# Layer norms centred on VectorE alone, attention weights loaded from ScalarE's queue, unread products at two places of the first layers

## The chip, the cores and the metric

One NeuronCore of a Trainium2 chip. The kernel is one program on one core; the metric is the time of one execution in microseconds, median over runs. All data is fp32 unless said otherwise.

## What is computed

x is 8 images of 64 channels, 16x16 pixels. Cut from the reference:

```python
x = L0(x)   # non-local block: theta, phi, g by 1x1 products (phi, g max-pooled 2x2)
            # f = softmax(theta^T phi); y = f g; w_y = Ww y; batch norm of w_y; + x
x = L1(x)   # sign(x+b11) conv 3x3 with sign weights, bn, + x, prelu;
            # sign, conv 1x1 with sign weights, bn, + , prelu
t = to_tokens(x)                      # 8 x 256 tokens of 64
t = t + attention8(ln(t))             # 8 heads, softmax, Wu, + bu
t = t + moe(ln(t), 8 experts, top 2)  # gelu
t = t + haar_attention(ln(t))         # keys by pinv(W_Q), rotary, Haar far field
t = t + moe(ln(t), 16 experts, top 2) # silu(h1) * h2
ln(v) = (v - mean(v)) / sqrt(var(v) + 1e-5)     # over the 64 of a token
```

## The kernel before

Each engine runs a program of its own, written out by hand, and the engines meet at semaphores. Nothing is scheduled: an engine's order is the order of its code, and an instruction that waits holds all behind it. The images lie in pairs on the 128 partitions (x0, 128x1024); the tokens in T, 16 tiles of 128 tokens by 64, on 128 partitions.

**The first layers (0 to 42 us).** SP issues all loads one after another: w0, x, vec, wwT, the conv weights (w3T, w1T, w3n, w1n), the loads for the pseudo-inverse (nsA, nsAT), consts (with the identity for transposes), then the five attention weights wqT, wkT, wvT, wu, bu on one semaphore `attn_loaded`, then the rest. TensorE computes w0 times x (L1204, four products of 512 columns; an fp32 product is two records in the trace), theta times phi (L1212), gw (L1220), then the fold of wkT and wqT (L1226, eight products into bank 7, behind `attn_loaded`), the transposes of f_prob (L1235), the wy products (L1242), five unread products (`keep_clock`, L836, 128x512 bf16 on the sign weights w3s), a join of the batch norm's halves (L1250), the fold of wvT and wu (L1254), eight more unread products, and the 3x3 conv (L1262). ScalarE: theta (L690), the sign weights (L697, L698), two exponentials (L702), two copies AH of the fold (L707), the copy of the first transposes (L710), wy (L713). VectorE: the softmax of f up to f_prob (L1482), sums of the conv weights (L1486 to L1489), the copy of the second transposes (L1491), AL from the fold (L1495), the counts of wy for the batch norm (L1500). GpSimd zeroes tiles first: phi, gw, sgn, w3s, w1s, then `zeros` (128x128).

**The layer norms.** There are four (n = 0 to 3), ahead of each attention and each expert layer, all by `layer_norm` on VectorE with helpers. VectorE takes the statistics of the 16 tiles (L1594), makes the mean (L1602) and the variance (L1603, L1604), and centres tiles 0 to 7 (L1605) while `ln_pool` on GpSimd centres tiles 8 to 15 (L478). ScalarE takes the square root (L600), VectorE the reciprocal (L1607) and multiplies the 16 tiles in four pieces (L1612), the third of which waits for GpSimd. TensorE transposes them piece by piece. In the first norm GpSimd then adds bu to T (L572). `step` makes VectorE wait for its own instruction.

Of the kernel before, what the change touches and what calls it, by code (L numbers as in the profile page):

```python
# [24 lines left out]
ALU = mybir.AluOpType  # L25
# [3 lines left out]
P = 128  # L29
B, C, IMG = 8, 64, 16  # L30
# [7 lines left out]
EXP2, EXP3, HID = 8, 16, 128  # L38
# [102 lines left out]
def hybrid_kernel(nc, io, out):  # L141
    ctx = ExitStack()
    with ctx:
# [5 lines left out]
        def S(name):  # L149

            if name not in sems:
                sems[name] = ctx.enter_context(nc.semaphore(name))
            return sems[name]
# [29 lines left out]
        wqT = from_early(C, HEADS * C).rearrange("p (h m) -> p h m", h=HEADS)  # L183
        wu = from_early(C, HEADS * C).rearrange("p (h m) -> p h m", h=HEADS)
# [226 lines left out]
        def _(sp):  # L411
            def load(dst, src, name):
                sp.dma_start(dst, src).then_inc(S(name), 16)
# [3 lines left out]
            load(vec[:], io["vec"], "vec_loaded")  # L417
            load(wwT[:], io["wwT"], "ww_loaded")
            load(w3T[:], io["w3T"], "l1_loaded")
# [7 lines left out]
            load(consts[:], io["consts"], "consts_loaded")  # L427
            load(wqT[:], io["wqT"], "attn_loaded")
            load(wkT[:], io["wkT"], "attn_loaded")
            load(wvT[:], io["wvT"], "attn_loaded")  # L430
            load(wu[:], io["wu"], "attn_loaded")
            load(bu[:], io["bu"], "attn_loaded")
            load(wq3[:], io["q3"], "l3_loaded")
# [39 lines left out]


        def ln_pool(gp, n):

            gp.wait_ge(S("ln_mean"), n + 1)
            gp.tensor_tensor(xn[:, 8:16], T[:, 8:16], lnc[:, 1, 8:16].unsqueeze(2).broadcast_to([P, 8, C]),  # L478
                             ALU.subtract).then_inc(S("ln_centred"), 1)

# [68 lines left out]
        @block.gpsimd  # L549
        def _(gp):  # L550
            gp.memset(phi[:], 0.0).then_inc(S("blocks_zeroed"), 1)
            gp.memset(gw[:], 0.0).then_inc(S("blocks_zeroed"), 1)
            gp.memset(sgn[:], 0.0).then_inc(S("pads_zeroed"), 1)
            gp.memset(w3s[:], 0.0).then_inc(S("pads_zeroed"), 1)
            gp.memset(w1s[:], 0.0).then_inc(S("pads_zeroed"), 1)
            gp.memset(zeros[:], 0.0).then_inc(S("zeros_ready"), 1)
            gp.wait_ge(S("zeros_ready"), 1)
            gp.memset(ones64[:], 1.0).then_inc(S("ones_ready"), 1)
            gp.memset(first_row[:], 0.0).then_inc(S("zeros_ready"), 1)
            gp.wait_ge(S("zeros_ready"), 2)  # L560
            for o in range(2):
                gp.memset(first_row[C * o:C * o + 1, o, :], 1.0).then_inc(S("ones_ready"), 1)
                gp.wait_ge(S("ones_ready"), o + 2)
            gp.memset(b2two[:], 0.0).then_inc(S("b2_zeroed"), 1)
            gp.memset(gates[:], 0.0).then_inc(S("gates_zeroed"), 1)

            gp.wait_ge(S("attn_loaded"), 80)
            ln_pool(gp, 0)
            gp.wait_ge(S("ln_normalised"), 4)
            for u in range(2):  # L570
                t8 = T[:, 8 * u:8 * u + 8, :]
                gp.tensor_tensor(t8, t8, bu[:].unsqueeze(1).broadcast_to([P, 8, C]),  # L572
                                 ALU.add).then_inc(S("t_biased"), 1)
            attention_pool(gp)
            ln_pool(gp, 1)
            ln_pool(gp, 2)
            l3_pool(gp)
            ln_pool(gp, 3)

            gp.wait_ge(S("f3_hid_ready"), CHUNKS)  # L580
            for kk in range(CHUNKS, CHUNKS * EXP3):
                e, c = kk // CHUNKS, kk % CHUNKS
                slot, filled = gate_slot(3, e)
                gp.wait_ge(S(f"gate_row{slot}_{c // 2}"), 16 * filled)
                gp.wait_ge(S("f3_glu"), kk + 1)
                gp.tensor_tensor(hid[kk % RING], hid[kk % RING], gate_rows[slot][:, c * CHUNK:(c + 1) * CHUNK],
                                 ALU.mult).then_inc(S("f3_hid_ready"), 1)
# [96 lines left out]
        def _(act):  # L684
            act.preload_act_table(ACT.Exp)
            act.wait_ge(S("vec_loaded"), 16)

# [4 lines left out]

            act.wait_ge(S("l1_loaded"), 64)
            act.wait_ge(S("pads_zeroed"), 3)
# [138 lines left out]
        def keep_clock(pe, bank, products):  # L833

            for _ in range(products):
                pe.matmul(ps[:, bank, :], w3s[:, 0, :], w3s[:, 4:8, :].rearrange("p k m -> p (k m)"), start=True, stop=True)  # L836
# [361 lines left out]
        @block.tensor  # L1198
        def _(pe):
            pe.wait_ge(S("l0_loaded"), 32)  # L1200

# [15 lines left out]
            pe.wait_ge(S("pg_ready"), 1)  # L1217
            pe.wait_ge(S("ww_loaded"), 16)
            for j in range(J):
# [3 lines left out]

            pe.wait_ge(S("attn_loaded"), 80)
            for h in range(HEADS):
                mm = pe.matmul(ps[:, 7, h * C:(h + 1) * C], wkT[:, h, :], wqT[:, h, :],  # L1226
                               start=True, stop=True)
            mm.then_inc(S("folded"), 1)

            pe.wait_ge(S("consts_loaded"), 16)  # L1230
# [8 lines left out]
            for j in range(J):  # L1239
# [4 lines left out]
                if j % 2 == 1:  # L1244
                    mm.then_inc(S("wy_ready"), 1)

            pe.wait_ge(S("wsign_ready"), 4)
            keep_clock(pe, 2, 5)
            pe.wait_ge(S("bn_halves"), 1)
            pe.matmul(ps[:, 6, 0:2], con("halfavg"), col[:, 0:2], start=True,  # L1250
                      stop=True).then_inc(S("bn_joined"), 1)

            for h in range(HEADS):
                mm = pe.matmul(ps[:, 3, h * C:(h + 1) * C], wvT[:, h, :], wu[:, h, :],  # L1254
                               start=True, stop=True)
# [182 lines left out]
        def _(dve):  # L1438
# [3 lines left out]
            def wide(c, n=C, t=TILES):  # L1442

                return c.unsqueeze(2).broadcast_to([P, t, n])
# [36 lines left out]
            for q in halves:  # L1481
                tt(f_prob[:, q], f_exp[:, q], wide(f_col[:, 2, q], t=8), ALU.mult).then_inc(S("f_prob_ready"), 1)  # L1482
            dve.wait_ge(S("l1_loaded"), 64)
            ones = [("w3n", w3n, 9 * C, 20), ("w1n", w1n, C, 21)]
# [104 lines left out]
            def layer_norm(n, after_first=None):  # L1589
# [11 lines left out]
                step(tt(lnc[:, 3, :], lnc[:, 1, :], lnc[:, 1, :], ALU.mult))  # L1601
                ts(lnc[:, 1, :], lnc[:, 0, :], 0.5, None, ALU.mult).then_inc(S("ln_mean"), 1)  # L1602
                step(stt(lnc[:, 4, :], lnc[:, 3, :], C / 4.0, lnc[:, 2, :], ALU.mult, ALU.add))  # L1603
                ts(lnc[:, 5, :], lnc[:, 4, :], 1.0 / C, EPS_LN, ALU.mult, ALU.add).then_inc(S("ln_var"), 1)  # L1604
                step(tt(xn[:, 0:8], T[:, 0:8], wide(lnc[:, 1, 0:8], t=8), ALU.subtract))  # L1605
                dve.wait_ge(S("ln_std"), n + 1)
                step(dve.reciprocal(lnc[:, 7, :], lnc[:, 6, :]))  # L1607
                for p in range(4):
                    q = slice(CT * p, CT * p + CT)
                    if p == 2:  # L1610
                        dve.wait_ge(S("ln_centred"), n + 1)
                    tt(xn[:, q], xn[:, q], wide(lnc[:, 7, q], t=CT), ALU.mult).then_inc(S("ln_normalised"), 1)  # L1612
# [248 lines left out]
```

## Time and profile before

| | |
|---|---|
| median of 3 runs | 397.25 us (395.0 to 397.92) |
| the profiled execution | 399.14 us |
| its span (first to last instruction) | 397.4 us |
| mean granted TensorE clock | 0.914 |
| busy: PE, PEld, DVE, ACT, POOL | 347.0, 237.8, 272.3, 211.7, 165.9 us |
| instructions | 7115 |

PE is TensorE's matmuls, PEld its weight loads, DVE VectorE, ACT ScalarE, POOL GpSimd, SPq SP's queue. A timeline row gives start and duration in us, then engine, line, operation, output <- input, and shapes; neighbours of one kind are merged (x8), and a bracket tells the idle time before it and what ended it. Full TensorE clock (1.0) is 2.4 GHz, 0.5 is 1.2 GHz.

### The profile page before, as it was taken

To read this page: it belongs to the slowest core of one execution; us is meant where nothing else is said; L and a number is where in the kernel's file an instruction comes from. 1 tells how busy PE (TensorE), PEld (TensorE's weight loads), DVE (VectorE), ACT (ScalarE), POOL (GpSimd) and SP (SyncE) were. 2 spreads that over 40 slices of the span, in tenths; PEclk is the share of its full clock that TensorE was granted. 3 is DMA by queue.
4 is the path that set the end of the run, shared out by engine and by line. 5 is a ranking of instruction groups with operands and counts; after the bars stand their busy time and mean duration, and the time that the engine had idled before them with its cause. 6 is when DMAs were issued, how large, how long until landed. Compare 5 with 4: busy or idle time off the path is not lost. (4 is left out here: it accounts for less than half of the span.)

```text
span 397.4 us, 7115 instructions
## 1 busy us (share of the span) xinstructions
PE 347.0 (87%) x2438; PEld 237.8 (60%) x2438; DVE 272.3 (69%) x657; ACT 211.7 (53%) x523; POOL 165.9 (42%) x175
## 2 busy tenths in 40 slices
PE   4786389999999999999769999858467899999996
PEld 1552266888888888887454233346055666666662
DVE  1878777888888888877383664687895655555541
ACT  1555358777777677878527444360324344444440
POOL 5000135455455545555310000140110299999995
PEclk9988559999999999999977999985578999999999
DMA  6944000000000000000000991000000946665531
GB/s 175 236 99 163 0 0 1 2 2 2 1 2 2 1 2 2 2 1 2 0 2 10 338 357 44 2 0 2 0 0 15 316 156 216 208 194 192 206 107 53
DMA packets 16436, 30.92 MB, mean 78 GB/s; under 512 B 5968, under 2 KB 9744, under 8 KB 16400
## 3 DMA queue, kind: packets, MB, share of 16 engines
q1 hardware_dynamic: 16400, 30.46, 23.9%
q8 instruction: 20, 0.33, 0.3%
q14 instruction: 16, 0.13, 0.1%
HBM read 29.73 MB, written 0.72 MB: 77 GB/s over the span
## 5 line engine op out<-in xcount | busy, mean ns | idle before, releaser
L524 POOL TENSOR_TENSOR va_vb<-va_vb,rowinv 128x512 f32<-128x512 f32 x64 | 66.6, 1041 | 70.1 <-DVE rowinv L1681 70.1
L649 ACT ACTIVATE va_vb<-ps,negmax 128x256 f32<-128x256 f32 x128 | 59.8, 477 | 8.0 <-DVE negmax L1674 7.8
L776 ACT ACTIVATE wy<-ps 128x512 f32<-128x512 f32 x64 | 38.1, 597 | 46.8 <-PE ps L1111 46.8
L1111 PE MATMUL ps<-XP,early 64*128 64x256 f32 x512 | 58.0, 380 | 1.5 <-DVE hid_g L1742 1.5
L1111 PEld LDWEIGHTS ps<-XP,early 64*128 64x128 f32 x512 | 46.6, 186 | 14.8 <-issue 5.5
L1674 DVE TENSOR_REDUCE negmax<-ps 128x2 f32<-128x512 f32 x64 | 44.1, 689 | 7.8 <-PE ps L912 7.6
L912 PE MATMUL ps<-keys_gates,xcur 128*128 128x256 f32 x256 | 47.9, 310 | 1.4 <-DVE keys_gates L1666 1.4
L478 POOL TENSOR_TENSOR xn<-T,lnc 128x512 f32<-128x512 f32 x4 | 4.2, 1042 | 105.7 <-DVE lnc L1602 105.7
L912 PEld LDWEIGHTS ps<-keys_gates,xcur 128*128 128x128 f32 x256 | 35.5, 195 | 13.8 <-issue 11.3
L923 PE MATMUL ps<-consts,va_vb 128*128 128x128 f32 x256 | 39.2, 276 | 2.8 <-POOL va_vb L524 2.3
L939 PE MATMUL ps<-pT,vproj 128*64 128x256 f32 x256 | 34.5, 392 | 0.0
L923 PEld LDWEIGHTS ps<-consts,va_vb 128*128 128x128 f32 x256 | 30.3, 148 | 6.7 <-POOL va_vb L524 4.2
L640 ACT ACTIVATE keys_gates<-ps 128x512 fp32r<-128x512 f32 x32 | 19.2, 600 | 27.2 <-PE ps L889 27.1
L649 ACT ACTIVATION_READ_ACCUMULATOR va_vb<-ps,negmax 128x1 f32 x128 | 26.5, 207 | 0.0
L1666 DVE TENSOR_TENSOR keys_gates<-ps,keys_gates 128x512 fp32r<-128x512 f32 x32 | 22.1, 691 | 3.7 <-ACT keys_gates L640 2.6
L633 DVE COPY pT<-ps 128x512 f32<-128x512 f32 x32 | 21.8, 682 | 1.9 <-PE ps L923 1.9
L1767 DVE TENSOR_TENSOR theta_qk<-ps,wy 128x512 f32<-128x512 f32 x16 | 11.1, 692 | 14.1 <-ACT wy L776 14.1
L939 PEld LDWEIGHTS ps<-pT,vproj 128*64 128x64 f32 x256 | 15.6, 136 | 7.6 <-issue 1.4
L1681 DVE RECIPROCAL rowinv<-rowsum 128x2 f32<-128x2 f32 x64 | 10.6, 166 | 13.7 <-ACT va_vb L649 13.3
L1051 PE MATMUL ps<-XP,w2raw 64*128 64x512 f32 x64 | 19.4, 688 | 0.0
L631 ACT ACTIVATE pT<-ps 128x512 f32<-128x512 f32 x32 | 19.3, 603 | 0.2 <-PE ps L923 0.2
L888 PE MATMUL ps<-xcur,AH 128*128 128x256 f32 x64 | 17.7, 297 | 0.1
(322 smaller groups left out, 684.5 us busy)
## 6 DMA issues: line engine op xcount, KB each, us to landing
pT<-gates_row SPq DMA_DIRECT2D x16, 512.0 KB, 4.8
vproj<-gates_row SPq DMA_DIRECT2D x14, 512.0 KB, 5.1
gate_row_keys<-gates_row SPq DMA_DIRECT2D x14, 512.0 KB, 4.9
early<-in_f_in SPq DMA_DIRECT2D x1, 2048.0 KB, 8.4
consts<-in_consts SPq DMA_DIRECT2D x1, 816.0 KB, 5.3
x<-in_x SPq DMA_DIRECT2D x1, 512.0 KB, 4.5
w2raw<-in_f_in SPq DMA_DIRECT2D x1, 512.0 KB, 4.0
out<-in_f_out SPq DMA_DIRECT2D x1, 512.0 KB
```

Of the source, the lines that this page charges most:

```text
L524: gp.tensor_tensor(prob[:, n % 4], prob[:, n % 4], rowinv[:, n % 4, :].unsqueeze(2).broadcast_to([P, U, N]), ALU.mult).then_inc(S("p_scale ...
L631: eng.activation(dst, src, ACT.Copy).then_inc(S("pT_even"), 1)
L633: eng.tensor_copy(dst, src).then_inc(S("pT_odd"), 1)
L649: ins = act.activation(prob[:, n % 4, u, :], ps[:, 1 + n % 2, u * N:(u + 1) * N], ACT.Exp, bias=negmax[:, n % 4, u:u + 1], accum_out=rowsu ...
L776: act.activation(act_out[:, kk % 2, :].rearrange("p (o n) -> p o n", o=2), ps[:, 2 * pair_of(kk):2 * pair_of(kk) + 2, 0:2 * P], ACT.Silu). ...
L912: mm = pe.matmul(ps[:, 1 + n % 2, u * N:(u + 1) * N], xcur[:, g, u * P:(u + 1) * P], K[:, k % 2, n % 2, :], start=(part == 0), stop=(part ...
L923: mm = pe.transpose(ps[:, 3 + n % 2, su * N + u * P:su * N + (u + 1) * P], prob[:, n % 4, u, su * P:(su + 1) * P], ident)
L939: mm = pe.matmul(ps[h * C:(h + 1) * C, 5, 0:N], vproj[:, g, su, head * C:(head + 1) * C], pT[:, (2 * k + h) % 4, su, :], start=(k % 4 == 0 ...
L1051: pe.matmul(ps[:, kk % 4, :], w2raw[r, e], pairs(c // 2)[r], start=True, stop=True).then_inc(S("f2_h_ready"), 1)
L1111: mm = pe.matmul(ps[:, 2 * pair_of(kk) + o, w * 2 * P:(w + 1) * 2 * P], w3raw[r, e, w * HID:(w + 1) * HID], pairs(c, 2)[r], start=True, st ...
L1666: tt(KL[:, k % 2].rearrange("p h n -> p (h n)"), ps[:, 0, :], KH[:, k % 2].rearrange("p h n -> p (h n)").bitcast(F32), ALU.subtract).then_ ...
L1674: dve.tensor_reduce(negmax[:, n % 4, :], ps[:, 1 + n % 2, :].rearrange("p (u n) -> p u n", u=U), AX.X, ALU.max, negate=True).then_inc(S("m ...
```

## The change

Three edits. (1) The layer norms: `ln_pool` and its semaphores are gone; VectorE makes the variance first, then the mean, then centres both halves. (2) The attention weights are issued by ScalarE, after w0 and x have landed, keys' weights first, on two semaphores (`keys_loaded` for wkT and wqT, `values_loaded` for wvT, wu, bu); wwT now counts on `l1_loaded`, so gw waits for all conv weights. (3) TensorE multiplies the zeroed tile by itself eight times ahead of its first layer (so `zeros` is GpSimd's first memset), and has seven unread products between the first fold and the transposes of f_prob.

```diff
@@ sync (SP)
-            load(wwT[:], io["wwT"], "ww_loaded")
+            load(wwT[:], io["wwT"], "l1_loaded")
-            load(wqT[:], io["wqT"], "attn_loaded")
-            load(wkT[:], io["wkT"], "attn_loaded")
-            load(wvT[:], io["wvT"], "attn_loaded")
-            load(wu[:], io["wu"], "attn_loaded")
-            load(bu[:], io["bu"], "attn_loaded")
@@ gpsimd
-        def ln_pool(gp, n):
-            gp.wait_ge(S("ln_mean"), n + 1)
-            gp.tensor_tensor(xn[:, 8:16], T[:, 8:16], lnc[:, 1, 8:16].unsqueeze(2).broadcast_to([P, 8, C]),
-                             ALU.subtract).then_inc(S("ln_centred"), 1)
+            gp.memset(zeros[:], 0.0).then_inc(S("zeros_ready"), 1)
             gp.memset(phi[:], 0.0).then_inc(S("blocks_zeroed"), 1)
...
-            gp.memset(zeros[:], 0.0).then_inc(S("zeros_ready"), 1)
-            gp.wait_ge(S("zeros_ready"), 1)
...
-            gp.wait_ge(S("attn_loaded"), 80)
-            ln_pool(gp, 0)
+            gp.wait_ge(S("values_loaded"), 48)
@@ scalar
             act.preload_act_table(ACT.Exp)
+            act.wait_ge(S("l0_loaded"), 32)
+            act.dma_start(wkT[:], io["wkT"]).then_inc(S("keys_loaded"), 16)
+            act.dma_start(wqT[:], io["wqT"]).then_inc(S("keys_loaded"), 16)
+            act.dma_start(wvT[:], io["wvT"]).then_inc(S("values_loaded"), 16)
+            act.dma_start(wu[:], io["wu"]).then_inc(S("values_loaded"), 16)
+            act.dma_start(bu[:], io["bu"]).then_inc(S("values_loaded"), 16)
@@ tensor
+            pe.wait_ge(S("zeros_ready"), 1)
+            for _ in range(8):
+                pe.matmul(ps[:, 7, 0:HID], zeros[:], zeros[:], start=True, stop=True)
             pe.wait_ge(S("l0_loaded"), 32)
...
-            pe.wait_ge(S("ww_loaded"), 16)
+            pe.wait_ge(S("l1_loaded"), 80)
...
-            pe.wait_ge(S("attn_loaded"), 80)
+            pe.wait_ge(S("keys_loaded"), 32)
...
             mm.then_inc(S("folded"), 1)
+            pe.wait_ge(S("wsign_ready"), 4)
+            keep_clock(pe, 2, 7)
...
-            pe.wait_ge(S("wsign_ready"), 4)
             keep_clock(pe, 2, 5)
...
+            pe.wait_ge(S("values_loaded"), 48)
@@ vector, layer_norm
-                ts(lnc[:, 1, :], lnc[:, 0, :], 0.5, None, ALU.mult).then_inc(S("ln_mean"), 1)
                 step(stt(lnc[:, 4, :], lnc[:, 3, :], C / 4.0, lnc[:, 2, :], ALU.mult, ALU.add))
                 ts(lnc[:, 5, :], lnc[:, 4, :], 1.0 / C, EPS_LN, ALU.mult, ALU.add).then_inc(S("ln_var"), 1)
-                step(tt(xn[:, 0:8], T[:, 0:8], wide(lnc[:, 1, 0:8], t=8), ALU.subtract))
+                step(ts(lnc[:, 1, :], lnc[:, 0, :], 0.5, None, ALU.mult))
+                for half in range(2):
+                    q = slice(8 * half, 8 * half + 8)
+                    ins = tt(xn[:, q], T[:, q], wide(lnc[:, 1, q], t=8), ALU.subtract)
+                step(ins)
...
-                    if p == 2:
-                        dve.wait_ge(S("ln_centred"), n + 1)
```

TensorE's queue from its first product to the wy products, before (row number, line, operation, output <- input, what it waits for):

```order
1 L1204 MATMUL ps<-x,early 128x512 [waits l0_loaded]
2 L1204 MATMUL ps<-x,early 128x512 x3
...
11 L1220 MATMUL ps<-early,pg_vsum 128x128 [waits ww_loaded,pg_ready]
12 L1220 MATMUL ps<-early,pg_vsum 128x128 x3
13 L1226 MATMUL ps<-early 128x64 [waits attn_loaded]
14 L1226 MATMUL ps<-early 128x64 x7
15 L1235 MATMUL ps<-consts,f_prob 128x128 [waits f_prob_ready,consts_loaded]
```

and in the changed kernel:

```order
1 L1192 MATMUL ps<-zeros 128x128 [waits zeros_ready]
2 L1192 MATMUL ps<-zeros 128x128 x7
3 L1197 MATMUL ps<-x,early 128x512 [waits l0_loaded]
4 L1197 MATMUL ps<-x,early 128x512 x3
...
13 L1213 MATMUL ps<-early,pg_vsum 128x128 [waits l1_loaded,pg_ready]
14 L1213 MATMUL ps<-early,pg_vsum 128x128 x3
15 L1219 MATMUL ps<-early 128x64 [waits keys_loaded]
16 L1219 MATMUL ps<-early 128x64 x7
17 L826 MATMUL ps<-w3s 128x512 [waits wsign_ready]
18 L826 MATMUL ps<-w3s 128x512 x6
19 L1230 MATMUL ps<-consts,f_prob 128x128 [waits f_prob_ready,consts_loaded]
```

Fifteen products are new, eight ahead of the first layer and seven ahead of the transposes, and the fold waits for two loads instead of five.

VectorE's queue in the first layer norm, from the squares on (lnc holds the columns of 16 numbers), before:

```order
69 L1601 TENSOR_TENSOR lnc<-lnc 128x16 [waits dve_step]
70 L1602 TENSOR_SCALAR lnc<-lnc 128x16 [waits dve_step]
71 L1603 SCALAR_TENSOR_TENSOR lnc<-lnc 128x16
72 L1604 TENSOR_SCALAR lnc<-lnc 128x16 [waits dve_step]
73 L1605 TENSOR_TENSOR xn<-T,lnc 128x512
74 L1607 RECIPROCAL lnc<-lnc 128x16 [waits ln_std,dve_step]
```

and in the changed kernel:

```order
69 L1596 TENSOR_TENSOR lnc<-lnc 128x16 [waits dve_step]
70 L1597 SCALAR_TENSOR_TENSOR lnc<-lnc 128x16 [waits dve_step]
71 L1598 TENSOR_SCALAR lnc<-lnc 128x16 [waits dve_step]
72 L1599 TENSOR_SCALAR lnc<-lnc 128x16
73 L1602 TENSOR_TENSOR xn<-T,lnc 128x512 [waits dve_step]
74 L1602 TENSOR_TENSOR xn<-T,lnc 128x512
75 L1605 RECIPROCAL lnc<-lnc 128x16 [waits ln_std,dve_step]
```

The mean has moved behind the variance, and a second centring of 128x512 stands ahead of the reciprocal.

## Rows read from the trace of the kernel before

**Rows 1.** Stretches: start:end, length, busy us (instructions) by engine, PEclk, DMA share.

```profile
19.10:22.50 3.40, 3.19 (x12) 2.46 (x11) 2.85 (x7) 1.32 (x3) 0.00 (x0) 0.51 1.16 199
...
36.50:60.00 23.50, 14.42 (x57) 11.19 (x58) 17.91 (x52) 11.48 (x24) 5.18 (x6) 0.50 0.00 0
60.50:195.00 134.50, 131.74 (x1057) 109.25 (x1057) 109.38 (x249) 101.87 (x332) 71.04 (x85) 1.00 0.01 2
```

**Rows 2.** Timeline: the memset of zeros, the first layer's records and weight loads.

```profile
3.92 0.21 POOL L556 MEMSET zeros<- 128x128 f32 x1
...
5.77 5.25 PE L1204 MATMUL ps<-x,early 128*128 128x512 f32 x8 [5.77 <-DMA x<-in_x]
...
7.63 0.34 PEld L1204 LDWEIGHTS ps<-x,early 128*128 128x128 f32 x1 [0.52 <-issue]
8.49 0.34 PEld L1204 LDWEIGHTS ps<-x,early 128*128 128x128 f32 x1 [0.52 <-issue]
9.13 0.19 PEld L1204 LDWEIGHTS ps<-x,early 128*128 128x128 f32 x1 [0.31 <-issue]
9.56 0.19 PEld L1204 LDWEIGHTS ps<-x,early 128*128 128x128 f32 x1 [0.24 <-issue]
```

**Rows 3.** Timeline of the front, 10 to 29 us, the rows that matter.

```profile
10.26 1.48 ACT L690 ACTIVATE theta_qk<-ps,vec 128x512 f32<-128x512 f32 x2 [8.24 <-PE ps L1204]
...
12.95 1.06 PE L1220 MATMUL ps<-early,pg_vsum 128*128 128x128 f32 x8
...
16.81 2.00 PE L1226 MATMUL ps<-early 64*128 64x64 f32 x16 [2.80 <-DMA bu<-in_bu]
...
17.58 1.29 DVE L1482 TENSOR_TENSOR f_prob<-f_both,f_col 128x512 f32<-128x512 f32 x2
...
18.73 1.61 PE L1235 MATMUL ps<-consts,f_prob 128*128 128x128 f32 x8
...
18.84 1.09 ACT L707 ACTIVATE AH<-ps 128x512 fp32r<-128x512 f32 x2 [3.01 <-PE ps L1226]
...
19.81 0.60 ACT L710 ACTIVATE probT_rot<-ps 128x512 f32<-128x512 f32 x1
...
20.01 0.15 DVE L1489 TENSOR_SCALAR col<-col 128x1 f32<-128x1 f32 x1
20.45 0.69 DVE L1491 COPY probT_rot<-ps 128x512 f32<-128x512 f32 x1 [0.29 <-PE ps L1235]
...
20.56 2.95 PE L1242 MATMUL ps<-probT_rot,early 128*128 128x256 f32 x8 [0.21 <-ACT probT_rot L710]
21.06 1.28 DVE L1495 SCALAR_TENSOR_TENSOR AL<-ps,AH 128x512 fp32r<-128x512 f32 x2
...
23.55 0.70 DVE L1500 BATCH_NORM_STATS2 bn<-ps 128x6 f32<-128x512 f32 x1 [0.21 <-PE ps L1242]
...
26.79 1.90 PE L836 MATMUL ps<-w3s 128*128 128x512 bf16 x8
```

**Rows 4.** Timeline of the first norm (45 us) and, below, the last.

```profile
45.43 1.54 DVE L1605 TENSOR_TENSOR xn<-T,lnc 128x512 f32<-128x512 f32 x1
...
292.14 0.17 DVE L1602 TENSOR_SCALAR lnc<-lnc 128x16 f32<-128x16 f32 x1
...
292.39 1.04 POOL L478 TENSOR_TENSOR xn<-T,lnc 128x512 f32<-128x512 f32 x1 [6.79 <-DVE lnc L1602]
...
292.42 1.04 DVE L1604 TENSOR_SCALAR lnc<-lnc 128x16 f32<-128x16 f32 x1
293.38 0.68 DVE L1605 TENSOR_TENSOR xn<-T,lnc 128x512 f32<-128x512 f32 x1
294.09 0.25 DVE L1607 RECIPROCAL lnc<-lnc 128x16 f32<-128x16 f32 x1
```

**Rows 5.** Timeline: SP's issue of bu.

```profile
10.53 0.58 SPq L413 DMA_DIRECT2D bu<-in_bu  x1
```

**Rows 6.** DMA issues: KB, and us from issue to landing.

```profile
early<-in_wvT SPq DMA_DIRECT2D x1, 256.0 KB, 6.5
```

More of the change, by code:

```diff
@@ L574, in _ @@
             attention_pool(gp)
-            ln_pool(gp, 1)
-            ln_pool(gp, 2)
             l3_pool(gp)
-            ln_pool(gp, 3)
             gp.wait_ge(S("f3_hid_ready"), CHUNKS)
@@ L691, in _ @@
                                bias=v_("bt")).then_inc(S("theta_ready"), 1)
-            act.wait_ge(S("l1_loaded"), 64)
+            act.wait_ge(S("l1_loaded"), 80)
             act.wait_ge(S("pads_zeroed"), 3)
@@ L1482, in _ @@
                 tt(f_prob[:, q], f_exp[:, q], wide(f_col[:, 2, q], t=8), ALU.mult).then_inc(S("f_prob_ready"), 1)
-            dve.wait_ge(S("l1_loaded"), 64)
+            dve.wait_ge(S("l1_loaded"), 80)
             ones = [("w3n", w3n, 9 * C, 20), ("w1n", w1n, C, 21)]
```

## The prediction

> **What bounds the kernel now.** I read three views. First the stretches with TensorE's clock [rows 1]: from 60.5 to 195 us TensorE is busy 131.74 of 134.50 us at full clock, so nothing that saves VectorE or ScalarE time in the middle can show. The change touches only the front (0 to 50 us) and the four layer norms, where the engines wait for one another in turn and a saved stretch should pass to the end one for one. Second the timeline of the front, to find which wait ends last at each place [rows 2, 3]. Third the timeline around the norms [rows 4]. The profiled span is 397.4 us; its execution took 399.14 us, 1.9 us above the 397.25 us median. I form differences on the span and take them off the median.
>
> **The norms.** Before, VectorE centres eight tiles and GpSimd the other eight, each 128x512, seemingly at the same time. The rows say otherwise [rows 4]. In the last norm GpSimd's instruction begins at 292.39 us and takes 1.04 us; VectorE's next instruction, on 16 numbers per partition, takes 1.04 us too, where its neighbour of the same size (L1602) took 0.17 us, and ends with GpSimd's, at 293.46 and 293.43 us. In the first norm that small instruction escapes, and it is the centring (L1605) that takes 1.54 us instead of 0.68 us. So GpSimd's half is not beside VectorE's, it is ahead of it. New order, in durations of these rows: from the start of the old L1602 (292.14 us) the scaled sum takes 0.20 us to the next start (0.17 us and the gap behind it), the variance line 0.09 us (the step from L1602 to L1603, which don't wait for each other), the mean moved behind it 0.21 us, the first centring 0.60 us (0.68 us less the 0.08 us by which neighbours overlap), the second 0.71 us: 1.81 us to the reciprocal, where the trace has 294.09 - 292.14 = 1.95 us. **Gain 0.14 us a norm, 0.6 us for four.** Nothing waits for GpSimd there any more, and its later work in the first norm (adding bu) still waits for the same products. ScalarE's square root sits inside the two centrings, as it sat inside the stall.
>
> The Trainium skill ("SBUF — State Buffer", section "Who interferes with whom") says that a VectorE instruction with two SBUF inputs and a GpSimd instruction that reads SBUF take turns, whole instruction by whole instruction. The trace agrees for the 1.54 us centring, and shows the small one-input instruction blocked as well, which that sentence alone doesn't cover. By the rule no serial half is lost, and the sum of the paragraph above stands; without it the second centring would be a new 0.6 us a norm.
>
> **The front: what waits.** TensorE's fold product of keys and queries (L1226) waits for all five attention weights on one semaphore, the last of which SP issues at 10.53 us [rows 5]. It starts at 16.81 us, 2.80 us idle, and runs 2.00 us. Behind it in the same queue stand the transposes of f_prob (L1235), whose first half VectorE has ready near 18.2 us but which start at 18.73 us. ScalarE's two copies AH wait for the fold, run 18.84 to 19.93 us, and the copy of the first transposes stands behind them: 19.81 us. Its output releases the wy products at 20.56 us [rows 3]. By then the clock has fallen: after the idle 2.80 us and the narrow fold products, 19.1 to 22.5 us has a granted clock of 0.51 [rows 1], the 1.2 GHz level, and four wy products take 2.95 us.
>
> **The front after.** ScalarE issues the five loads itself after x has landed (5.77 us [rows 2]). An issue on SP takes about 0.6 us [rows 5], so its queue is free by about 8.7 us; theta, the next thing in it, starts at 10.26 us before [rows 3], so 1.5 us of cover hides the issues. Gone is that cover if the first layer ran at full clock (its third product, six records at 0.43 us, ends near 8.4 us, and theta could start near 8.5 us): then 0.2 us. Landing took up to 6.5 us from issue; wkT and wqT are issued by 6.9 us and land by 13.4 us at the latest, by that row [rows 6]. TensorE ends the gw products (L1220) near 14.0 us [rows 3], so the fold runs 14.0 to 16.0 us and seven unread products 16.0 to 17.6 us (the eight like them at L836 took 1.90 us [rows 3]); the sign weights that they read are written right behind theta. f_prob's first half comes at 18.2 us: the queue is free.
>
> From there, step by step. First transposes 18.3 to 18.8 us. ScalarE has made AH long before, so the copy runs 18.9 to 19.5 us instead of 19.81 to 20.41 us. But VectorE ends L1489 at 20.16 us whatever happens and now starts its own copy (L1491) at 20.2 us instead of 20.45 us. It then makes AL, 1.28 us, before it may count wy: so the first count can start at about 22.1 us, the second at 22.75 us instead of 23.55 us. The wy products at full clock (0.21 us a 256-column record instead of 0.43 us, half the steps of [rows 2]) are done by 20.6 and 21.9 us. All these starts of before are in [rows 3]. **VectorE is late next; gain 0.8 us**, not the 1.5 us that TensorE gains. If the clock stays low all the same, the second pair of products, from 20.9 us, ends near 22.7 us, still ahead of VectorE's 22.75 us, so the gain hardly shrinks; the lower bound is the 0.25 us by which L1491 starts sooner, the upper bound, in an execution where VectorE waits longer for a low clock, TensorE's 1.5 us.
>
> **The products on zeros.** Eight 128x128 fp32 products are sixteen records. The first layer's 512-column records start 0.86 us apart at the low clock [rows 2], so a 128-column record should take 0.21 us, and they run from about 1.1 us (zeros is now GpSimd's first memset, 0.21 us [rows 2], from about 0.7 us) to 4.6 us. Then TensorE idles 1.2 us until x lands. What do they buy? The weight loads of the first layer stand at 7.63 and 8.49 us, 0.86 us apart, and at 9.13 and 9.56 us, 0.43 us apart [rows 2]: it runs at 1.2 GHz for 3 us after work starts, then at 2.4 GHz, though the clock column says 1.00 there. Other rises in this trace came after 3.4 us of nearly unbroken work (19.1 to 22.5 us) and only at 60 us in a stretch with 14.42 us of broken work in 23.5 us [rows 1]. 3.5 us of work followed by 1.2 us of none lies at the low edge of that. I take nothing for it; the bounds are 0 and 3.4 us (eight records at 0.43 instead of 0.85 us), 1.6 us against this particular trace. It can't delay x: the products end first.
>
> The Trainium skill ("TensorE: Matmul & The Clock Gate", section "The HAM clock gate (the "warmup" mystery)") says that sustained work releases the clock and that the phase of this differs between executions. No row here shows a second phase. By that rule alone the same kernel would sometimes get the whole gain and sometimes none.
>
> **Sum.** 0.6 + 0.8 + 0 = 1.4 us: 397.25 - 1.4 = 395.8 us. Own range 395.0 to 396.6 us.
>
> **Rivals.**
> A. The zero products do raise the clock for the first layer. For it: they last as long as the shortest rises above. Against: the idle 1.2 us behind them. Gain 1.4 + 1.6 to 1.4 + 3.2 us, so 394.2 to 392.6 us; take 393.6 us. Chance 0.30.
> B. The later clock moves. Between 36.5 and 60 us the clock is 0.50 over 23.5 us, TensorE busy 14.42 us of it [rows 1]. If the work ahead of 60 us, now 1 us earlier, brings the rise sooner by as much as the shortest low stretch lasts, 3.4 us, those 3.4 us of work halve: 1.7 us more, 394.1 us. By the same size it may come later, 397.5 us. Chance 0.15, faster way mostly.
> C. Slower: the keys' weights come late. The fold and the seven products stand ahead of the transposes; the order decides against the change once the fold starts after 14.7 us. If sharing the DMA engines with consts, in flight at the same time, makes wkT land at 16.8 us, as bu does now, the fold ends at 18.8 us and the seven products, at the low clock 3.0 us, at 21.8 us: the transposes start 3.1 us later than 18.73 us; less 0.6 us of the norms, +2.5 us, 399.8 us. Against: even the longest landing of these rows, 6.5 us, gives 13.4 us [rows 6]. Chance 0.07; a smaller lateness gives 397 to 399.
> D. The edits do nothing measurable: x lands and VectorE's chain decide the front, and the norms' stall is of another origin, so that the second centring is added (+0.6 us a norm, +2.4 us, less 0.8): 398.9 us. Against: the 1.04 us ends 0.03 us after GpSimd's in the last norm [rows 4], and the same pair stands in the second and third. Chance 0.06.
>
> **Numbers.** The main case 0.42, A 0.30, B 0.15, C 0.07, D 0.06. Within 1% (3.97 us, about what a measurement of this kernel can tell) lie the main case, B, D, C and most of A; A together with B, or A on a median of slow starts, passes 1%: faster 0.20, same 0.76, slower 0.04. The range takes A's middle and a late clock: 392.6 to 397.8 us.
>
> **What would show it.** In the new profile: the first layer's weight loads 0.86 or 0.43 us apart; the fold starting right behind gw, near 14 us, and clock 1.00 from 16 to 29 us; VectorE going from AL straight to its counts without idle; in each norm 1.8 us from the squares to the reciprocal with no instruction on 16 numbers above 0.2 us. The prediction is wrong if the fold starts after 14.7 us, if theta waits for ScalarE's issues, or if the time of conv and attention changes through the clock by more than the 1.4 us summed.

## The result and the profile after

| | before | after |
|---|---|---|
| median, 6 runs each | 397.59 us (395.0 to 400.45) | 394.23 us (392.79 to 395.99) |
| the profiled execution | 399.14 us | 395.99 us |
| its span | 397.4 us | 394.2 us |
| mean granted clock | 0.914 | 0.918 |

The ratio of after to before is 0.990 (95%: 0.9867 to 0.9933): 3.4 us less. A second set of 12 runs of the same kernel gave 0.9909 (0.9879 to 0.9939). The forecast of 395.8 us was 1.6 us too long, inside the range; whether the gain passes 1% is left open by both intervals.

The timeline of after, its first 27 us. Columns as ahead of the prediction: start, duration, engine, line, operation; in the bracket the idle time and what ended it.

```profile
0.73 0.20 POOL L540 MEMSET zeros<- 128x128 f32 x1 [0.29 <-POOLq L1847]
...
0.99 3.78 PE L1192 MATMUL ps<-zeros 128*128 128x128 f32 x16 [0.99 <-POOL zeros L540]
...
4.89 0.57 ACTq L671 DMA_DIRECT2D early<-in_wkT  x1
...
4.92 4.12 PE L1197 MATMUL ps<-x,early 128*128 128x512 f32 x8
...
5.87 0.19 PEld L1197 LDWEIGHTS ps<-x,early 128*128 128x128 f32 x1 [0.46 <-issue]
...
6.30 0.19 PEld L1197 LDWEIGHTS ps<-x,early 128*128 128x128 f32 x1 [0.24 <-issue]
...
7.43 0.61 ACTq L675 DMA_DIRECT2D bu<-in_bu  x1
...
8.28 1.48 ACT L680 ACTIVATE theta_qk<-ps,vec 128x512 f32<-128x512 f32 x2 [6.26 <-PE ps L1197]
...
11.96 2.00 PE L1219 MATMUL ps<-early 64*128 64x64 f32 x16
...
14.11 1.46 PE L826 MATMUL ps<-w3s 128*128 128x512 bf16 x6 [0.16 <-issue]
...
16.44 1.17 PE L1230 MATMUL ps<-consts,f_prob 128*128 128x128 f32 x8 [0.87 <-DVE f_prob L1477]
...
17.85 2.25 PE L1237 MATMUL ps<-probT_rot,early 128*128 128x256 f32 x8 [0.24 <-ACT probT_rot L700]
...
18.83 1.28 DVE L1490 SCALAR_TENSOR_TENSOR AL<-ps,AH 128x512 fp32r<-128x512 f32 x2
...
20.03 1.29 DVE L1495 BATCH_NORM_STATS2 bn<-ps 128x6 f32<-128x512 f32 x2
...
21.61 0.38 PE L1244 MATMUL ps<-col,consts 128*128 128x2 f32 x2 [0.43 <-DVE col L1497]
...
26.54 4.22 PE L1257 MATMUL ps<-sgn,w3s 128*128 128x512 bf16 x18 [0.79 <-ACT sgn L713]
```

Three things are to be seen. The first layer (L1197) takes 4.12 us instead of 5.25 [rows 2], its weight loads from 5.87 us on lie 0.43 us apart: from there it runs at 2.4 GHz. The fold (L1219) waits for no transfer; before, it waited 2.80 us, until bu had landed at 16.81 us [rows 3]. And VectorE goes from AL (ends at 20.11 us) into its two counts with no idle time.

The fourth norm in the same kernel, in VectorE's timeline. It answers to [rows 4].

```profile
288.98 0.17 DVE L1597 SCALAR_TENSOR_TENSOR lnc<-lnc 128x16 f32<-128x16 f32 x1
289.19 0.17 DVE L1598 TENSOR_SCALAR lnc<-lnc 128x16 f32<-128x16 f32 x1
289.27 0.17 DVE L1599 TENSOR_SCALAR lnc<-lnc 128x16 f32<-128x16 f32 x1
289.48 1.29 DVE L1602 TENSOR_TENSOR xn<-T,lnc 128x512 f32<-128x512 f32 x2
290.81 0.25 DVE L1605 RECIPROCAL lnc<-lnc 128x16 f32<-128x16 f32 x1
```

The small instructions take 0.17 us each, where one took 1.04 us before. From L1597 to the reciprocal it is 1.83 us, in all four norms; it was 1.95 us.

The join of the batch norm's halves (L1244 in after) stands in the timeline of before at

```profile
24.55 0.38 PE L1250 MATMUL ps<-col,consts 128*128 128x2 f32 x2
```

**Where the 3.2 us of span lie.** x landed at 4.92 us instead of 5.77: 0.85 us. From x to theta it is 3.36 us instead of 4.49 (10.26 - 5.77): 1.13 us. From theta to the join it is 0.96 us less (13.33 instead of 14.29), and the conv begins 2.95 us earlier, at 26.54 instead of 29.49 us. Four norms give 0.5 us; 0.2 us is lost again behind the conv, less than the pieces of the next section move by. The part of x isn't counted for the change: x landed between 4.97 and 5.77 us in the five profiles of this study without products ahead of the first layer, and between 4.92 and 5.24 us in the eight with them. The ranges overlap; that both late landings (5.52 and 5.77 us) are among the five may be chance, and no run decides it.

### The profile page after: what moved, and what is told of

It is laid out like the page before. It is cut to its first block and busy times, and to the rows that moved or that the text cites. A ratio compares the mean times of both kernels' runs of the same rounds, so it can differ in the third digit from the quotient of the medians.

```text
span 394.2 us, 7158 instructions
## 1 busy us (share of the span) xinstructions
PE 349.9 (89%) x2458; PEld 240.1 (61%) x2461; DVE 271.4 (69%) x661; ACT 211.5 (54%) x523; POOL 161.5 (41%) x171
## 5 line engine op out<-in xcount | busy, mean ns | idle before, releaser
L498 POOL TENSOR_TENSOR va_vb<-theta_qk,consts 128x512 f32<-128x512 f32 x2 | 2.5, 1268 | 66.9 <-ACT theta_qk L784 66.9
L617 DVE COPY pT<-ps 128x512 f32<-128x512 f32 x32 | 21.8, 682 | 1.9 <-PE ps L913 1.9
L1041 PE MATMUL ps<-XP,w2raw 64*128 64x512 f32 x64 | 19.4, 685 | 0.0
L559 POOL TENSOR_TENSOR T<-T,bu 128x512 f32<-128x512 f32 x2 | 2.5, 1268 | 39.7 <-DVE xn L1608 39.7
```

Source lines behind the costliest of these rows:

```text
L617: eng.tensor_copy(dst, src).then_inc(S("pT_odd"), 1)
L1041: pe.matmul(ps[:, kk % 4, :], w2raw[r, e], pairs(c // 2)[r], start=True, stop=True).then_inc(S("f2_h_ready"), 1)
```

## One execution against another

The study's kernels carry the same work from the conv on, norms and unread products aside. Cut into pieces, each execution that was profiled has these lengths in us (the borders are x's landing, the conv's first product, and the reciprocals of norms 2, 3 and 4):

| kernel | x to conv | conv to norm 2 | norm 2 to 3 | norm 3 to 4 | norm 4 to end |
|---|---|---|---|---|---|
| before | 23.7 | 173.7 | 53.5 | 37.4 | 103.3 |
| norms_only (its front is that of before) | 25.6 | 172.7 | 52.3 | 37.3 | 102.8 |
| after | 21.6 | 173.7 | 53.3 | 37.3 | 103.4 |
| after_again (the same code) | 21.6 | 173.5 | 53.4 | 37.2 | 103.5 |
| front_only | 21.7 | 172.8 | 52.4 | 35.9 | 102.7 |
| zeros13 (x by 5.17 us, see there) | 21.7 | 172.3 | 53.3 | 37.3 | 103.4 |
| no_zeros | 23.3 | 172.0 | 53.2 | 37.3 | 103.2 |
| no_seven | 22.3 | 172.9 | 52.3 | 37.3 | 103.1 |
| loads_only | 23.2 | 173.7 | 52.4 | 35.8 | 102.8 |
| zeros_only | 26.9 | 172.9 | 52.6 | 37.4 | 102.7 |
| seven_only | 28.6 | 172.7 | 52.4 | 35.8 | 102.7 |
| warm_middle | 21.6 | 172.0 | 52.3 | 35.7 | 102.7 |
| warm_norms | 21.8 | 171.6 | 51.5 | 35.7 | 102.7 |

The later pieces come at two or three lengths, and their own code doesn't decide which: norm 3 to 4 takes 37.4 or 35.8 us with the old norms (before, front_only), and 37.3 or 35.7 us with the new ones (after, warm_middle). The one kernel profiled twice, after and after_again, shows the same lengths within 0.2 us; both executions were the slowest of their sets of 6 and 12. That equal code does vary is shown by the twelve timed executions of after_again: 391.78 to 396.19 us, at mean granted clocks between 0.918 and 0.939. The stretches show what differs; the columns are start:end, length, busy us of PE, PEld, DVE, ACT and POOL, the granted clock, and the DMA share with GB/s. After, from the conv to norm 2 and from norm 3 to 4:

```profile
26.54:200.26 173.72, 156.21 (x1186) 126.20 (x1186) 139.06 (x347) 119.99 (x365) 75.15 (x90) 0.93 0.04 12
...
253.53:290.81 37.28, 23.49 (x169) 14.98 (x169) 30.88 (x86) 12.04 (x28) 6.84 (x5) 0.63 0.00 1
```

The same two in front_only:

```profile
26.75:199.57 172.82, 153.94 (x1186) 123.82 (x1186) 139.22 (x346) 119.22 (x365) 77.36 (x92) 0.95 0.04 12
...
251.95:287.80 35.85, 22.23 (x169) 13.85 (x169) 31.03 (x85) 11.23 (x28) 7.89 (x6) 0.68 0.00 1
```

The counts of records are equal (1186 and 169); front_only was granted the full clock for more of the stretch, and TensorE needed 2.3 and 1.3 us less for the same products. Between 30 and 62 us the clock stood at 0.50 for 23.9 us in before, after and after_again, for 20.5 us in loads_only, for 17.1 us in norms_only and front_only and for 13.6 us in zeros13. So pieces that no edit touched move the span of one execution by 3 to 4 us, and the 6 us between the fastest and the slowest run of one kernel are in keeping with that. Whether an edit ahead of a piece tips it to one length or the other, single profiles can't tell. The experiments are therefore read twice: by the piece of the profile that the edit touches, and by the median of many runs, never by the span of one profile.

## Experiments

Ratios are to the kernel before on the same chip, whose median there was 397.7 to 398.3 us over 23 to 32 runs. A ratio is not the quotient of the two medians: for loads_only and no_seven the medians alone would give 0.993 and 0.992 instead of 0.995 and 0.9942.

### Each edit alone

**norms_only.** The kernel before with the edit of the norms and nothing else.

```diff
+                step(ts(lnc[:, 1, :], lnc[:, 0, :], 0.5, None, ALU.mult))
+                for half in range(2):
+                    q = slice(8 * half, 8 * half + 8)
+                    ins = tt(xn[:, q], T[:, q], wide(lnc[:, 1, q], t=8), ALU.subtract)
+                step(ins)
```

> The kernel before with the norms' edit alone: VectorE centres both halves, the rest as before. Theory (GpSimd's centring and VectorE's work take turns): 1.83 us instead of 1.95 us from the end of the squares to the reciprocal in each of four norms, so 0.5 us less in all, ratio about 0.999. Rival (the halves ran side by side and the second centring is added): 2.4 us more, ratio 1.006.

Measured 397.85 us, ratio 0.9994 (0.9966 to 1.0021). VectorE's timeline of its first norm:

```profile
46.26 0.17 DVE L1592 SCALAR_TENSOR_TENSOR lnc<-lnc 128x16 f32<-128x16 f32 x1
46.46 0.17 DVE L1593 TENSOR_SCALAR lnc<-lnc 128x16 f32<-128x16 f32 x1
46.55 0.17 DVE L1594 TENSOR_SCALAR lnc<-lnc 128x16 f32<-128x16 f32 x1
46.75 1.29 DVE L1597 TENSOR_TENSOR xn<-T,lnc 128x512 f32<-128x512 f32 x2
48.08 0.25 DVE L1600 RECIPROCAL lnc<-lnc 128x16 f32<-128x16 f32 x1
```

1.82 us by these rows. The second centring is not added to the old path: that rules out the rival by which four norms would lose 2.4 us (0.6%), which also lies outside the interval. The 0.5 us that the profile shows (0.1%) can't be told from nothing in the time.

**loads_only.** The kernel before with the five weights issued by ScalarE, the two semaphores, and wwT counted on `l1_loaded`; no product added.

```diff
+            act.wait_ge(S("l0_loaded"), 32)
+            act.dma_start(wkT[:], io["wkT"]).then_inc(S("keys_loaded"), 16)
...
-            pe.wait_ge(S("attn_loaded"), 80)
+            pe.wait_ge(S("keys_loaded"), 32)
```

> The kernel before with the attention weights issued by ScalarE on two semaphores and nothing else (no zero products, no seven products, norms split with GpSimd). Theory: the fold starts right behind gw at about 14 us after the same start of the first layer, AL and the counts are bound by VectorE, 0.5 to 0.8 us less. Rival (the seven products carry the gain through the clock): wy products still at 0.43 us a record and the counts hardly earlier, 0.3 us or less.

Measured 395.59 us, ratio 0.995 (0.9927 to 0.9972): 2.0 us (1.1 to 2.9), more than the 0.5 to 0.8 us of the theory and far from the rival's 0.3 us. TensorE's timeline of its front:

```profile
13.61 2.00 PE L1226 MATMUL ps<-early 64*128 64x64 f32 x16
18.09 1.52 PE L1235 MATMUL ps<-consts,f_prob 128*128 128x128 f32 x8 [2.48 <-DVE f_prob L1483]
19.49 3.28 PE L1242 MATMUL ps<-probT_rot,early 128*128 128x256 f32 x8
```

The fold starts at 13.61 us behind gw, so the transfer's wait is gone by this edit alone. But TensorE now idles 2.48 us ahead of the transposes, and the wy products take 3.28 us, at the lower clock, as before. x to conv is 23.2 us, 0.5 us under the profile of before and 2.4 us under norms_only's, which has the same front. The timed 2.0 us fit between these two; how often each of the two comes, no run here shows.

**zeros_only.** The kernel before with the eight products on zeros, and `zeros` as GpSimd's first memset.

```diff
+            pe.wait_ge(S("zeros_ready"), 1)
+            for _ in range(8):
+                pe.matmul(ps[:, 7, 0:HID], zeros[:], zeros[:], start=True, stop=True)
```

> The kernel before with the eight products on zeros and the earlier memset alone. Theory (the zero products raise the clock during the first layer in many executions): the first layer's weight loads go from 0.86 to 0.43 us apart at its first or second load, theta starts 3.4 us after x lands instead of 4.5 us, 1.1 us or more less in the median. Rival (the short first layer of the changed kernel was chance of one execution): theta 4.5 us or more after x, ratio 1.000.

Measured 397.74 us, ratio 1.0008 (0.9981 to 1.0035): nothing, where the theory expected 1.1 us or more in the median. The first layer did get shorter (x at 5.13, theta at 8.37 us: 3.24 us). Then TensorE's timeline:

```profile
16.86 3.67 PE L1228 MATMUL ps<-early 64*128 64x64 f32 x16 [4.75 <-DMA bu<-in_bu]
20.47 1.97 PE L1237 MATMUL ps<-consts,f_prob 128*128 128x128 f32 x8
22.36 3.75 PE L1244 MATMUL ps<-probT_rot,early 128*128 128x256 f32 x8
```

bu lands when it did, so the fold still starts at 16.86 us. The gain ahead of it has become idle time, 4.75 us instead of 2.80, and within the longer idle time, at 16.0 us, the clock had already fallen: the fold takes 3.67 us instead of 2.00 and the wy products 3.75 instead of 2.95 [rows 3]. x to conv was 26.9 us, the longest but one. **The first layer's 1.1 us are worth nothing that the time can show as long as the fold behind it waits for bu.**

**seven_only.** The kernel before with the seven unread products behind its late fold.

```diff
+            pe.wait_ge(S("wsign_ready"), 4)
+            keep_clock(pe, 2, 7)
```

> The kernel before with the seven unread products between the first fold and the transposes, and nothing else, so they stand behind a fold that starts at 16.8 us. Theory (they are free only where the queue would wait for f_prob anyway): transposes start 1.5 us later, at 20.3 us or more, the counts about 1 us later, ratio 1.001 to 1.004. Rival (what they do for the clock of the wy products pays for their own time): ratio 0.998 to 1.000.

Measured 399.22 us, ratio 1.0042 (1.0009 to 1.0076): slower, 1.7 us. TensorE's timeline:

```profile
16.84 3.67 PE L1226 MATMUL ps<-early 64*128 64x64 f32 x16 [3.19 <-DMA bu<-in_bu]
20.44 0.61 PE L836 MATMUL ps<-w3s 128*128 128x512 bf16 x1
21.27 2.34 PE L836 MATMUL ps<-w3s 128*128 128x512 bf16 x5 [0.22 <-issue]
23.40 1.92 PE L1237 MATMUL ps<-consts,f_prob 128*128 128x128 f32 x8
```

and the stretch around it, granted clock 0.50:

```profile
16.00:26.00 10.00, 8.94 (x32) 6.82 (x34) 4.22 (x10) 1.68 (x3) 0.00 (x0) 0.50 0.66 133
```

This is rival C's mechanism as it would look: the fold late, the products in front of the transposes at half speed, and f_prob's first half, ready near 17.9 us, waiting for a start at 23.40 us. The fold's own 3.67 us are not the seven products' doing: the clock had fallen at 15.7 us, in the wait for bu, ahead of them. zeros_only's profile has the same slow fold at the same place and no products behind it; its conv begins at 32.08 us, and here at 33.74 us, 1.7 us later, as much as the time lost.

### The change without one of its parts

**front_only** (the change with the old norms), **no_zeros** (without the eight), **no_seven** (without the seven), **zeros13** (thirteen instead of eight).

```diff
@@ no_seven
-            pe.wait_ge(S("wsign_ready"), 4)
-            keep_clock(pe, 2, 7)
@@ zeros13
-            for _ in range(8):
+            for _ in range(13):
```

> The changed kernel with the norms of before (GpSimd centres half): loads, zero products and seven products together. Theory: all of the gain but the norms' 0.5 us, so 2.9 us less than before, ratio 0.993. Rival (the norms carry more than their own chains, through the clock): ratio 0.996 or above.

Measured 394.88 us, ratio 0.991 (0.9875 to 0.9944). The two intervals don't tell it from the whole change (0.990): as far as time shows, the gain is the front's.

> The changed kernel without the eight products on zeros. Theory (they raise the clock for the first layer): it loses 1 us or more against the changed kernel, first layer's weight loads 0.86 us apart for 3 us or longer, ratio to before about 0.994. Rival (they do nothing): the same time as the changed kernel, ratio 0.990 to 0.991.

Measured 395.24 us, ratio 0.992 (0.9893 to 0.9946). In the profile the zeros are worth 1.7 us: x to conv is 23.3 us without and 21.6 us with them. In time it is 0.1 to 0.2%, and the intervals overlap. One reason that the profile offers: the clock came back earlier in this execution, and conv to norm 2 took 172.0 us instead of 173.7. Whether products early in the front shift that later rise, or chance did, one execution can't tell; that stays open. This kernel is the main case of the forecast, in which the products on zeros do nothing, and it gained 3.2 us (2.1 to 4.3).

> The changed kernel without the seven unread products between the fold and the transposes. Theory (VectorE is the next bound there): the clock falls between 14 and 20 us, wy records take 0.43 us, but VectorE's counts start less than 0.4 us later, ratio to before 0.991. Rival (the clock carries the gain): 0.8 to 1.5 us lost, ratio 0.993 to 0.994.

Measured 395.19 us, ratio 0.9942 (0.9914 to 0.9969), so 0.3 to 0.4% of gain are missing, more than VectorE's chain seemed to leave. TensorE's timeline, and one stretch of it:

```profile
12.18 2.00 PE L1219 MATMUL ps<-early 64*128 64x64 f32 x16
16.66 1.21 PE L1228 MATMUL ps<-consts,f_prob 128*128 128x128 f32 x8 [2.48 <-DVE f_prob L1476]
18.07 3.44 PE L1235 MATMUL ps<-probT_rot,early 128*128 128x256 f32 x8 [0.20 <-ACT probT_rot L700]
```

```profile
18.00:20.00 2.00, 1.93 (x5) 1.60 (x6) 1.90 (x6) 0.00 (x0) 0.00 (x0) 0.50 1.10 197
```

After the narrow fold, 2.48 us of idle time and most of the transposes the clock falls to 0.50 at 17.7 us, just ahead of the wy products; they take 3.44 us instead of 2.25, end at 21.51 us, and VectorE waits for the second half. x to conv is 22.3 us against 21.6: 0.7 us. With the seven products the idle time is 0.87 us and the clock stays at 1.00 throughout. The timed loss of 1.3 to 1.7 us, by the ratios, is larger than those 0.7 us; but by the medians it is 0.4 to 0.6 us, and the intervals overlap, so the time doesn't show it.

> The changed kernel with thirteen products on zeros instead of eight, so that TensorE works without a pause from 1 us until x has landed. Theory (what the first layer lacks is unbroken work): all its weight loads stand 0.43 us apart in every profile; the last zero products may hold the first layer back by up to 1 us after x; about the time of the changed kernel with less spread, ratio 0.988 to 0.991. Rival (zero products don't count towards the clock): loads 0.86 us apart at first and the first layer 1 us later, ratio 0.993.

Measured 394.58 us, ratio 0.9903 (0.9867 to 0.9939): the same as with eight. The weight loads are 0.43 us apart from the second on; behind eight products they are so from the second, the third or (warm_norms) the fourth on. The profile also shows a cost. ScalarE's first issue and TensorE's first layer wait for the same two loads:

```profile
5.17 0.54 ACTq L671 DMA_DIRECT2D early<-in_wkT  x1
...
5.77 3.60 PE L1197 MATMUL ps<-x,early 128*128 128x512 f32 x8
```

x had landed by 5.17 us, and TensorE, still on zeros, began 0.6 us late. Its first layer is shorter (3.60 us), so that theta starts 3.45 us after the landing, as with eight.

### What is left: the middle

In after the clock is low from 33.1 to 57 us. **warm_middle** puts 36 more unread products into TensorE's waits there: 13 ahead of the 1x1 convs, 4 and 19 ahead of the first norm's transposes. **warm_norms** adds 14 ahead of the second norm's transposes, and 6 and 8 in the far-field attention. **after_again** is the change, unedited, beside it.

```diff
@@ warm_middle
+                keep_clock(pe, 6, (6, 7)[p])
...
+                if p == 0:
+                    keep_clock(pe, 1, 4)
+            keep_clock(pe, 1, 19)
@@ warm_norms, besides
+            keep_clock(pe, 5, 6)
...
+            keep_clock(pe, 5, 8)
...
+            keep_clock(pe, 2, 14)
```

> The changed kernel with 36 more unread products in TensorE's idle time between the 3x3 conv and the first norm's transposes (6 and 7 ahead of the two 1x1 products, 4 and 19 around the second transposes of x2). Theory (the stretch from 33 to 57 us runs at 1.2 GHz because TensorE pauses): the clock stays at 1.00 there, the first norm's transposes take 2 us instead of 3.6 us and the first attention steps less, 2 to 5 us less than the changed kernel, ratio to before 0.978 to 0.985. Rival (VectorE and ScalarE bound that stretch): clock 1.00 but 1 us or less, ratio 0.988.

Measured 391.43 us (390.48 to 393.81), ratio 0.983 (0.9794 to 0.9866): 6.8 us faster than the kernel before on that chip. The change itself gained 3.4 and 3.6 us in its two sets of runs, not taken beside this one. Its two stretches from 30 to 60 us:

```profile
30.00:45.00 15.00, 11.91 (x60) 5.69 (x59) 13.28 (x42) 7.64 (x12) 0.00 (x0) 1.00 0.12 38
45.00:60.00 15.00, 11.95 (x66) 9.88 (x65) 11.43 (x27) 9.50 (x27) 6.24 (x7) 0.77 0.01 2
```

The same two of after:

```profile
30.00:45.00 15.00, 5.15 (x20) 2.95 (x19) 12.82 (x41) 7.70 (x12) 0.00 (x0) 0.60 0.10 33
45.00:60.00 15.00, 13.36 (x63) 10.80 (x62) 10.77 (x25) 8.57 (x22) 5.68 (x7) 0.60 0.00 1
```

And the norm's transposes in TensorE's timeline of warm_middle, behind the nineteen products:

```profile
39.27 4.26 PE L826 MATMUL ps<-w3s 128*128 128x512 bf16 x19
44.46 1.94 PE L834 MATMUL ps<-consts,xn 128*64 128x128 f32 x16 [0.92 <-DVE xn L1612]
```

In after they are

```profile
44.70 3.62 PE L834 MATMUL ps<-consts,xn 128*64 128x128 f32 x16 [5.03 <-DVE xn L1608]
```

The products fill what was a wait for VectorE of 5.03 us, and the sixteen transposes then take 1.94 us. The clock falls only at 49 us, for 6.8 us instead of 23.9. From the conv to norm 2 it is 172.0 us instead of 173.7 and 173.5. But no_zeros has 172.0 us there without these products, so this piece alone doesn't show the gain; the time of six runs does, all of them at or below 393.81 us. How much of it lies in the later pieces, which were short in this execution, stays open.

> The changed kernel once more, on the chip and in the rounds of the two below. Theory: ratio 0.990 again, x lands anywhere between 4.9 and 5.8 us, the first layer's weight loads 0.43 us apart from the second or third on, theta about 3.4 us after x. Rival (the first profile was a lucky phase of the clock): loads 0.86 us apart and theta 4.5 us after x in this one.

Measured 394.03 us, ratio 0.9909 (0.9879 to 0.9939); theta began 3.35 us after x, 3.36 us in the first profile.

> The kernel warm_middle with 28 more unread products: 14 ahead of the second norm's transposes, 6 and 8 in TensorE's pauses of the Haar attention. Theory (TensorE's queue is full behind the second norm, at half clock from 201 to 210 us): clock 1.00 there, the gate and the first hidden layers 3 to 4 us shorter, the Haar part 0 to 1 us, ratio to before 0.972 to 0.978. Rival (the chain through VectorE bounds that stretch too): ratio 0.981 to 0.983, as warm_middle.

Measured 391.58 us (390.32 to 392.39), ratio 0.9848 (0.9806 to 0.989): the same as warm_middle, so the further gain that my theory expected isn't there, though the mean clock rose from 0.943 to 0.974. The mean clocks are those of the two profiled executions. TensorE's timeline of its second norm:

```profile
196.32 2.97 PE L826 MATMUL ps<-w3s 128*128 128x512 bf16 x13 [0.16 <-issue]
199.33 1.44 PE L838 MATMUL ps<-consts,xn 128*128 128x128 f32 x8
...
202.13 1.99 PE L1041 MATMUL ps<-XP,w2raw 64*128 64x512 f32 x8
205.47 1.09 PE L863 MATMUL ps<-consts,gates 128*128 128x128 f32 x8 [1.35 <-DVE gates L1647]
```

In after L1041's eight records take 3.78 us, at the low clock, and L863 waits for nothing. Here they take 1.99 us, but L863 then waits 1.35 us for VectorE's gates. Norm 2 to 3 was 51.5 us, 0.7 us under the best of the others, and the six runs don't show it in time. warm_middle is the version to keep of these.

## Why the prediction was right, and where it was wrong

**The norms: right.** 0.14 us a norm was worked out, 0.12 us measured, and the stall of a 16-number instruction is gone with GpSimd's part. The Trainium skill ("SBUF — State Buffer", section "Who interferes with whom") has the two engines take turns at a shared port. The trace agrees: 1.04 us for the small instruction beside GpSimd, 0.17 us without. In the time the norms' 0.5 us can't be seen (norms_only).

**The front's waits: right in the profile, short in the time.** The fold runs right behind gw, ScalarE's five issues end at 8.04 us, 0.24 us ahead of theta (the 0.2 us of cover named for a fast first layer), the seven products lie inside the wait for f_prob, the clock column says 1.00 through to 33 us, and VectorE's AL and counts are the next bound. 0.8 us was the forecast from theta on, 0.96 us the profile's measure. Against the other length of the front of before (25.6 us from x to conv) it is more; I had taken the one profile of before for the kernel. Timed, the loads alone gained 2.0 us (1.1 to 2.9), and the front without the zeros, with the norms, 3.2 us (2.1 to 4.3), where 0.8 and 1.4 us were forecast.

**The zeros: a term that was mis-sized.** "I take nothing for it" is the step that the profiles contradict. It measured 1.13 us from x to theta. All eight profiles with the products have theta 3.2 to 3.55 us after x, all five without them 4.4 to 5.6 us. In the time it is small: 0.4 to 0.8 us between no_zeros and the change, with intervals that overlap. The reason given against it was an idle 1.2 us before x lands; x landed earlier in nearly every profile of the study, and behind eight products the idle time was 0.15 to 0.75 us; the longest, in no_seven, went with a first layer as quick as the others (theta 3.29 us after x). What 1.2 us would do wasn't seen. This is rival A. It priced the zeros at 1.6 us and more; the first records still ran slow (the third weight load stands 0.95 us behind the start), which leaves 1.13 us. The Trainium skill ("TensorE: Matmul & The Clock Gate", section "The HAM clock gate (the "warmup" mystery)") says that the number of slow products at a kernel's start differs between executions. The traces of the five kernels without the zeros agree with it, one execution each (1.2 us of spread); none shows an execution in which the zeros had not helped.

**The sum.** 0.5 + 0.96 + 1.13 = 2.6 us by the profiles' pieces, against 3.4 us timed and 1.4 us forecast. The measured 394.23 us lies outside the main case's own range (395.0 to 396.6 us); the stated range held it because it took in rival A, and rival A's cause is not the larger part of the miss, since no_zeros gained 3.2 us without it. So the hit of the range is in part luck. What the rest is stays open. It may be the other length of the front of before (1.9 us longer), where x lands, or the later clock. For the clock speaks that the executions of before were granted 0.916 to 0.917 on average (74 of them), those of the change 0.925 (6) and 0.929 (12): by these numbers and the spans, an estimated 66 us at the low clock against 59 and 56 us. The front of before accounts for 3.4 us of that in its profile and for 6.8 us in norms_only's. Rival B, that the later clock moves, is therefore not refuted; its size, 1.7 us, is also what single executions differ by. Rivals C and D are refuted by the start of the fold (11.96 us) and by norms_only.

## What to carry to other kernels

Put unread products only where TensorE waits for another engine anyway and products that the chain needs follow soon. The 36 in the middle did pay (0.983 against 0.990 and 0.991). The same seven cost 0.4% behind a late fold; behind an early one they kept the wy products at the full clock (2.25 us instead of 3.44), for a gain that the time doesn't show clear of noise. Time saved ahead of a wait that still ends when it did (bu at 16.8 us) came back as longer idle time, and in the profile of zeros_only as a lower clock. Before pricing an edit from one profile, look at more than one execution, and at where the profiled one lies among the timed ones; the twelve runs of after_again differ by 1.1% with no edit at all.

## What the runs showed of the hardware

- With 3.5 to 3.8 us of fp32 products on zeros that ended 0.15 to 0.75 us before the first real one, the weight loads of the first layer stood 0.43 us apart, the 2.4 GHz spacing, from its second, third or fourth on, in seven profiles of seven; thirteen products (4.95 us) brought theta no sooner.
- At the start of a kernel the clock column can't be trusted: it says 1.00 while the weight loads of the first layer lie 0.86 us apart [rows 2], which the same loads 0.43 us apart in after show to be half speed.
- Narrow fp32 products (64 columns) followed by 2.48 us of idle time were followed by a fall of the clock in no_seven; with seven 512-column products between and 0.87 us of idle time, it stayed.
- A stretch with the same code was granted the full clock for more or less of its time: 37.4 or 35.8 us between norms 3 and 4 with the old norms (before, front_only), 37.3 or 35.7 us with the new ones (after, warm_middle).
